# Who multiplies delta by x: VectorE's 24 products go to GpSimd, and six convolution taps move behind the first halves

## The reference, cut to what matters

```python
xc = silu(conv3x3_depthwise(xh) + conv_b)              # DI = 192 channels, 32 x 32, 4 images
x_flat = xc.reshape(B, DI, L)                          # by rows
x_t = jnp.transpose(xc, (0, 1, 3, 2)).reshape(B, DI, L)  # by columns
xs = concatenate([x_hwwh, flip(x_hwwh)], 1)            # K = 4 orders
x_dbl = jnp.einsum('bkdl,kcd->bkcl', xs, x_proj_w)
dts, Bs, Cs = jnp.split(x_dbl, [R, R + N], axis=2)
dts = softplus(einsum('bkrl,kdr->bkdl', dts, dt_projs_w) + dt_projs_b)
# scan over L, N = 16 states: d = dts, u = xs
h = h * exp(d_t[..., None] * As) + (d_t * u_t)[..., None] * B_t[:, :, None, :]
y = einsum('bkcn,bkn->bkc', h, C_t)
```

## Time and profile before

| | |
|---|---|
| median of three runs | 2246.07 us (2244.6 to 2247.19) |
| profiled execution, span from first to last instruction | 2244.7 us (its device time is not given apart) |
| VectorE, ScalarE, GpSimd busy in the span | 1575.2, 1144.9, 1297.0 us |
| mean granted TensorE clock | 0.968 |
| delta stage on ScalarE's queue, first `dt_out` | from 95.37 us |
| half 7's first instruction on VectorE | 153.21 us |
| first multiplication of the scans on VectorE | 253.46 us |

### The profile page before, as it was taken

How to read it: one execution, slowest core, us unless ns; L and a number is a source line. 1 busy time by engine, 2 the same in 40 slices (tenths; PEclk the granted TensorE clock), 3 DMA queues, 4 the chain that set the end, 5 groups by cost and what they waited for, 6 DMA issues and landing times.

```text
span 2244.7 us, 20167 instructions
## 1 busy us (share of the span) xinstructions
PE 1984.1 (88%) x5826; PEld 919.6 (41%) x5830; DVE 1575.2 (70%) x1505; ACT 1144.9 (51%) x1258; POOL 1297.0 (58%) x464
## 2 busy tenths in 40 slices
PE   7988588888888888888888888989995999999997
PEld 3332133333333333333333333456653555555554
DVE  6978999999999999999999999774553000000000
ACT  4788666666776676776767666211213112122111
POOL 0110499999999999999999999401233011111110
PEclk9987599999999999999999999999997999999999
DMA  6448622233222233222232220611226233333300
GB/s 193 151 175 280 212 75 75 70 98 79 84 66 65 75 100 91 65 75 75 61 105 67 77 73 19 229 42 57 85 85 223 85 119 124 123 119 126 126 24 7
DMA packets 82402, 229.13 MB, mean 102 GB/s; under 512 B 14031, under 2 KB 40257, under 8 KB 80816
## 3 DMA queue, kind: packets, MB, share of 16 engines
q1 hardware_dynamic: 76208, 211.54, 29.6%
q0 software_dynamic: 6144, 16.98, 2.1%
HBM read 166.39 MB, written 64.03 MB: 103 GB/s over the span
## 4 chain that ended last, share of the span: by engine, by line
PE 46%; DVE 23%; issue 17%; POOL 8%; ACT 3%; DMA 1%; DVEq 0%; SPq 0%; ACTq 0%; POOLq 0%
DVE arena L1705 15%; PE ps L1489 11%; PE ps L1502 11%; PE ps L1229 6%; POOL arena L604 4%; POOL arena L587 4%; PE ps L1439 3%; PE ps L1213 2%; PE ps L1110 2%; DVE ps L1688 1%; PE ps L1226 1%; PE ps L1139 1%; PE ps L1390 1%; PE ps L1428 1%; DVE arena L1572 1%
## 5 line engine op out<-in xcount | busy, mean ns | idle before, releaser
L604 POOL TENSOR_TENSOR arena<-arena 128x2048 f32<-128x2048 f32 x192 | 868.3, 4533 | 16.6 <-DVE arena L1705 15.7
L1229 PE MATMUL ps<-arena 128*128 128x512 f32 x1536 | 727.7, 596 | 27.7 <-POOL arena L604 27.6
L1705 DVE TENSOR_TENSOR_SCAN arena<-arena,ps 128x1024 f32<-128x1024 f32 x264 | 587.5, 2266 | 0.0
L880 ACT ACTIVATE arena<-ps 128x1024 f32<-128x1024 f32 x384 | 390.7, 1017 | 248.0 <-PE ps L1213 246.1
L1213 PE MATMUL ps<-arena 96*128 (+1 forms) x1296 | 366.7, 384 | 129.3 <-DVE arena L1705 112.7
L1229 PEld LDWEIGHTS ps<-arena 128*128 128x128 f32 x1536 | 288.4, 190 | 287.7 <-issue 194.0
L587 POOL TENSOR_TENSOR arena<-arena 128x1024 f32<-128x1024 f32 x120 | 283.1, 2359 | 103.5 <-DMA arena<-b_rows 103.5
L2066 DVE TENSOR_TENSOR arena<-ps,arena 128x384 f32<-128x384 f32 x32 | 17.8, 557 | 450.4 <-PE ps L1502 450.4
L1688 DVE TENSOR_TENSOR ps<-ps,arena 128x1024 f32<-128x1024 f32 x264 | 309.1, 1216 | 12.6 <-PE ps L1213 12.6
L873 ACT ACTIVATE arena<-arena 128x1024 f32<-128x1024 f32 x264 | 300.8, 1139 | 8.9 <-DVE arena L1705 8.3
L1213 PEld LDWEIGHTS ps<-arena 96*128 96x128 bf16 x1296 | 112.9, 98 | 461.3 <-DVE arena L1705 215.7
(11 more groups left out here) (225 smaller groups left out, 1611.9 us busy)
## 6 DMA issues: line engine op xcount, KB each, us to landing
arena<-b_rows SPq DMA_DIRECT2D x240, 256.0 KB, 4.2
arena<-in_w SPq DMA_DIRECT2D x16, 2304.0 KB, 13.3
delta<-arena SPq DMA_DIRECT2D x24, 512.0 KB, 2.9
delta_x<-arena SPq DMA_DIRECT2D x24, 512.0 KB, 3.1
arena<-delta SPq DMA_DIRECT2D x24, 512.0 KB, 3.6
arena<-delta_x SPq DMA_DIRECT2D x24, 512.0 KB, 4.6
slot_in<-arena SPq DMA_DIRECT2D x8, 772.0 KB, 8.1
arena<-slot_in SPq DMA_DIRECT2D x8, 772.0 KB, 18.0
```

Source lines behind the costliest of these rows:

```text
L604: nc.gpsimd.tensor_tensor(hst[:, h:h + 2], hst[:, h:h + 2], c_sb[:, c:c + 2], ALU.mult).then_inc(p2_ok, 2)
L880: nc.scalar.activation(c_sb[:, u % RING], C_PS, ACT.Copy).then_inc(c_free, 1)
L1229: mm = pe.matmul(Y_PS[:, h * 512:(h + 1) * 512], ident, hst[:, u % HRING, h * 512:(h + 1) * 512], start=False, stop=(u == UN - 1))
L1705: nc.vector.tensor_tensor_scan(h, f, x, 0.0, ALU.mult, ALU.add).then_inc(sc_ok, 1)
```

## The change

GpSimd now makes all 24 products of delta and x (`delta_x`), each as soon as delta is ready; VectorE's `finish` ends with delta. The three copies by columns of the second pair, which stood ahead, are put behind the products of halves 7, 8 and 9 in GpSimd's queue. On VectorE 12 of the second pair's 20 taps remain before the first half, six stand at the ends of steps 0, 1 and 2, two each, and the two that follow TensorE's taps stay at the end of step 5. The instructions are the same, and none but the 24 products changes its engine.

```diff
-LAST_TAPS_AT = 5
+BY_COLUMNS_BEHIND = (7, 8, 9)
+TAPS_FIRST, TAPS_AT = 12, {0: 2, 1: 2, 2: 2, 5: 2}
...
+            def delta_x(p, i):
+                k, j, q, dr = half_of(p, i)
+                m = p * HALVES + i
+                d, u = d_mk[:, m % MADE], u_mk[:, m % MADE]
+                pool.wait_ge(d_ok, m + 1)
+                nc.gpsimd.tensor_tensor(u, d, xy[:, q, :], ALU.mult).then_inc(du_ok, 1)
+
+            for j in range(J):
+                by_columns(0, j)
             for p in range(NP):
-                for j in range(J):
-                    by_columns(p, j)
+                for i in range(HALVES):
+                    delta_x(p, i)
+                    if p == 0 and i in BY_COLUMNS_BEHIND:
+                        by_columns(1, BY_COLUMNS_BEHIND.index(i))
...
                 nc.vector.tensor_tensor(d, d, u, ALU.subtract).then_inc(d_ok, 1)
-                if k == 1:
-                    dve.wait_ge(xT_ok, (p + 1) * J)
-                dve.wait_ge(d_ok, m + 1)
-                nc.vector.tensor_tensor(u, d, xy[:, q, :], ALU.mult).then_inc(du_ok, 1)
...
-            whole_third(0)
-            whole_third(1)
+            done = 0
             for p in range(NP):
                 for s in range(HALVES + 1):
+                    if p == 0 and s == 0:
+                        for n in range(TAPS_FIRST):
+                            second_pair_tap(n)
+                        done = TAPS_FIRST
                     if s < HALVES:
                         lost_part(p, s)
                     if s >= 1:
                         finish(p, s - 1)
-                    if p == 0 and s == LAST_TAPS_AT:
-                        last_taps(J - 1)
+                    if p == 0 and s in TAPS_AT:
+                        for n in range(done, done + TAPS_AT[s]):
+                            second_pair_tap(n)
+                        done += TAPS_AT[s]
```

More of the change, by code:

```diff
@@ L1577, in taps, with whole_tap @@
                         chain.link(ins)
-            def whole_third(j):
+            def whole_tap(j, tap):
                 acc = xy[:, OJ + j, :].rearrange("p (h w) -> p h w", w=HW)
[L1582 to L1591, removed]
@@ L1593, in last_taps @@
-            def last_taps(j):
-                slot = fill_slot("conv", 1, j).rearrange("p (h w) -> p h w", w=HW)
[L1596 to L1606, removed]
+                dy, dx = divmod(tap, 3)
@@ new lines, in whole_tap @@
+                if tap == 0:
+                    dve.wait_ge(xh_ok, IN_ORDER.index((3, j)) + 1)
+                    chain.link(nc.vector.tensor_scalar(acc, xpad[:, j, 0:HW, 0:HW], conv_w[:, j, 0:1], None, ALU.mult))
+                    return
+                ins = nc.vector.scalar_tensor_tensor(out=acc, in0=xpad[:, j, dy:dy + HW, dx:dx + HW], scalar=conv_w[:, j, tap:tap + 1],
+                                                     in1=acc, op0=ALU.mult, op1=ALU.add)
+                if tap == TAPS - 1:
+                    ins.then_inc(conv_ok, 1)
+                else:
+                    chain.link(ins)
@@ new lines, in last_tap @@
+            def last_tap(j, tap):
+                slot = fill_slot("conv", 1, j).rearrange("p (h w) -> p h w", w=HW)
+                if tap == PE_TAPS:
+                    dve.wait_ge(cpe_ok, 1)
+                dy, dx = divmod(tap, 3)
+                last = tap == TAPS - 1
+                acc = xy[:, OJ + j, :].rearrange("p (h w) -> p h w", w=HW) if last else slot
+                ins = nc.vector.scalar_tensor_tensor(out=acc, in0=xpad[:, j, dy:dy + HW, dx:dx + HW], scalar=conv_w[:, j, tap:tap + 1],
+                                                     in1=slot, op0=ALU.mult, op1=ALU.add)
+                if last:
+                    ins.then_inc(conv_ok, 1)
+                else:
+                    chain.link(ins)
@@ L1608, in lost_part, with second_pair_tap @@
+            def second_pair_tap(n):
+                j, tap = divmod(n, TAPS)
+                if j < J - 1:
+                    whole_tap(j, tap)
+                else:
+                    last_tap(j, PE_TAPS + tap)
             def lost_part(p, i):
```

## The result

The changed kernel takes 2260.86 us (median of 4 runs, 2258.88 to 2264.46), the kernel before 2245.34 beside it (4 runs, 2244.08 to 2247.19). The ratio is 1.0072 with an interval of 1.0058 to 1.0086: slower by 15.5 us by the medians, where 13.8 were forecast. The profiled execution is the fastest of the four: 2258.88 us, with a span of 2257.1 and a granted clock of 0.968.

The account below looks back on a forecast made before the run. VectorE was taken to set the pace from 153 us on, with ScalarE not far behind. First stretch 0.5, second 12.6 and scans' start 0.7 sum to 13.8 us; 2246.07 + 13.8 = 2260, range 2252 to 2268 (8 in 10).

Parts of the forecast that it names:

- The hold: Delta stage: while both engines read SBUF operands, each GpSimd product costs VectorE 2.13 us, each copy 1.65.
- The second stretch: From half 7's first VectorE instruction to the end of half 23's product: 100.26 us becomes 112.9, 12.6 more.
- Covered at nothing: Delta stage: stores that now wait for GpSimd cost nothing, as buffer reuse takes 9.3 us of 13.2.
- The first stretch: Delta stage before half 7: the change makes it 0.5 us later, between 0 and 2.
- the walk: VectorE from 107.45 to the last tap's end, counted with five holds: 140.09 becomes 146.6.
- The scans' start: Start of the scans: GpSimd's first row is 0.7 us late for the third scan, between 0 and 2.5.
- No hold: Rival, second stretch: GpSimd's products cost VectorE nothing, ScalarE bounds it at 92 us, 8 us won: 2238; chance 8%.
- The ring: Rival, delta stage: ScalarE waits for buffers still to be stored, 1 us in each of 17 halves: 2277; chance 8%.
- Part of the hold falls into waits: Rival, delta stage: GpSimd runs partly while VectorE waits for ScalarE, loss 1.05 to 1.58 a product: 2246; chance 6%.

Follow-up runs that it names:

- e2: The changed kernel with the taps as before, so only the products and copies are moved: 2258.53 us, ratio 1.0058.
- e4: The kernel before plus 24 unneeded GpSimd products (x by x, 1024 columns), the second pair's copies behind the sixth: 2271.73 us, ratio 1.0121.
- e3: The changed kernel with the products left out: GpSimd writes zeros in their place and reads nothing; 2245.33 us, ratio 0.9999.
- e6: The changed kernel with SyncE's store of the second pair's first B and C parts one half earlier: 2257.28 us, ratio 1.0054.
- e8: The kernel before with only the last of the 24 products on GpSimd and the parts' store one half earlier: 2241.04 us, ratio 0.9987.
- e7: e3 (products left out) with the parts' store one half earlier, as in e6: 2242.30 us, ratio 0.9990 to the kernel before.

## Why the prediction was right, and where it was not

**The hold: right in kind, 2.03 instead of 2.13 a product.** Beside a product a VectorE instruction with two inputs mostly takes 3.24 to 3.26, at most 3.38. A copy cost 1.69 to 1.75, where 1.65 was forecast. e2 and e4 show that it is the products, e3 that it is their reading. The Trainium skill, page "SBUF — State Buffer", section "Who interferes with whom", says that VectorE with two SBUF inputs contends with a GpSimd instruction that reads SBUF and not with one that only writes it; e3 agrees with its 1.22 beside memsets. The price is a little under the other's whole duration, 2.03 of 2.36 and 0.87 of 1.04, for the reason that the prediction gives: part of the held instruction's start lies under the wait.

**The second stretch: 14.7 instead of 12.6, by two misses that nearly cancel.** Forecast were 36.2 + 5.0 = 41.2 of holds; measured are 35.5, since each is a little cheaper, one product met no instruction at all, and three met L1638 (2.43 to 2.52 for 0.69, 1.8 lost) and one met an instruction that came late (1.87 for 1.22). It was forecast that the waits of 5.6 vanish; 7.6 stand there. With both numbers from the trace the sum is 100.26 - 5.6 - 23.0 + 35.5 + 7.6 = 114.8, and 114.98 was measured. That the forecast came within 2.1 us is in part luck.

**The step that failed is "Covered at nothing".** It named the next half's stores behind the product's store on SyncE's queue, and checked the buffers' ring. It did not name the stores of the parts and of the rows of B that stand there too. Their wait could have been read in the view of the earlier trace rows, in one of the lines that were passed over; ScalarE's waits of before, 150 to 254:

```profile
ACT arena L747 <- issue: 2.2, 1, 2.2
```

With the product's store ahead of them later, it became 6.2, VectorE was held up for 4.16 and 1.64, and e6 took that away. What the wait costs net is 2.7 in e6's profile, as a hold takes part of its place.

**The first stretch can't be told from one profile.** Half 7 began 1.7 us earlier, not 0.5 later. TensorE's granted clock was higher: from 95 to 104 us 1.00 (the upper of its two levels, 2.4 GHz) where it had been 0.81 in the mean, and 0.79 instead of 0.68 up to 120. From 90 to 95 us both executions have it at 1.00 with TensorE busy throughout, so why it then fell in one of them stays open. e6, which runs the same code up to there, began half 7 at 155.50 with a mean of 0.88 over 95 to 137, the changed kernel at 151.55 with 0.92. These 4 us lie between two executions of the same code. At one mean clock the kernels differ, too. Up to there e8 is the kernel before, and it began half 7 at 151.58, 3.9 before e6. The rows from 95 to 137 us, e8 and then e6 (the clock is the third number from the end):

```profile
95.00:137.00 42.00, 40.17 (x81) 15.56 (x81) 37.58 (x33) 31.58 (x33) 0.00 (x0) 0.88 0.43 152
95.00:137.00 42.00, 40.18 (x81) 15.65 (x81) 32.63 (x24) 32.38 (x33) 9.39 (x3) 0.88 0.32 107
```

That would be more than the 0.5 of the forecast and its bound of 2, but it is one profile of each, so what the first stretch costs stays open.

One step of the walk through it was wrong: it took five holds. The fifth product met the taps that follow TensorE's, which have one operand in PSUM, and held nothing:

```profile
139.77 1.28 DVE L1614 SCALAR_TENSOR_TENSOR ps<-arena,ps 128x1024 f32<-128x1024 f32 x1
139.93 2.36 POOL L584 TENSOR_TENSOR arena<-arena 128x1024 f32<-128x1024 f32 x1 [3.55 <-DVE arena L1651]
```

From half 1's first instruction to the end of the last tap it is 36.3 us instead of 32.6, so 3.7 more, where the walk gave 6.5; with four holds of 2.0 it gives 3.8.

**The scans' start.** The third scan is 1.2 us late, where 0.7 was forecast; that is inside the bounds of 0 to 2.5.

**The rivals.** "No hold" was priced too high. e3 is that case and gains nothing, e7 2 us, not 8: the 92 us of the stretch took ScalarE as never waiting, but it waits 6.7 + 4.1 for stores, and 92 + 10.8 = 102.8, an estimate, is near e3's 101.1; the same sum with e7's 5.3 gives 97.3, and 95.4 was measured. At the scans' start GpSimd's rows are late in both, too: the third scan waits 2.2 in e3 and 2.1 in e7. The ring, a rival beside the hold, binds just where the hold is gone: with VectorE at 6.6 us a half there was room for it. Of the 20 GpSimd instructions in the stretch one fell wholly into a wait ("Part of the hold falls into waits").

## What to carry to other kernels

An idle GpSimd is no free place for an elementwise product while VectorE works on two SBUF operands: here it saved VectorE an estimated 1.28 us and cost it 2.03. Look for the few places where the two already met, and compare the long instructions there with the median of their line. When a step is handed to another engine, list everything behind its semaphore on every queue, SyncE's other stores too, and read each line of that engine's waits; and ask of each wait you remove whether something that was hidden in it will come out.

## What the hardware showed beyond that

- An instruction with one SBUF input, the addition of a constant (L1638), is held too: 2.52 instead of 0.69 at 156.36, where GpSimd's product had started at 155.98. It alone is also lengthened by memsets (1.09, 1.28 and 0.95 in e3). The Trainium skill, page "SBUF — State Buffer", section "Who interferes with whom", has `tensor_scalar` among the operations that can enter a two-port mode and then contend; the rows agree that it contends.
- The two engines hand over instruction by instruction, in the order of issue. At 165.98, when GpSimd's product ended, VectorE's instruction issued at 163.69 went ahead of the copy issued at 165.92; at 167.07 the copy went ahead of VectorE's next one, issued at 167.10. So here two GpSimd instructions in a row cost two VectorE instructions, not one.
- The hold does not show as idle time. In the changed kernel GpSimd's 18 products from 150 to 270 have a mean of 2.76 for an undisturbed 2.34, and VectorE, "busy" for 106.37 of 114.98 us, spends 35.5 of them standing.
